# A separate buffer for the scaled activation, two roots moved, and feed-forward constants computed later: one post-norm transformer layer

## The reference

```python
x = layernorm(x + attention(x))     # 16 heads of 64, causal, softmax, W_out, b_out
x = layernorm(x + ffn(x))
def ffn(x):
    h = layernorm(x) * ln_gamma + ln_beta
    y = silu(h @ dequant(fc1_q, fc1_scales) + fc1_bias)     # 256 -> 1024
    return x + 0.5 * (y @ dequant(fc2_q, fc2_scales) + fc2_bias)     # 1024 -> 256
```

## Time and profile before

| | |
|---|---|
| median of 3 runs | 1814.26 us (1811.79 to 1815.73) |
| the profiled execution | 1813.47 us, of which the profile's span is 1811.4 us |
| PE busy | 1697.7 us (94%) |
| ACT busy | 1567.0 us (87%) |
| DVE busy | 1377.2 us (76%) |
| POOL busy | 1359.9 us (75%) |
| the chain that ended last | PE 66%; ACT 19%; POOL 5%; DVE 5%; issue 4% |
| attention | to about 1484 us |
| feed-forward | the rest, about 327 us |

### The profile page before, as it was taken

The page is one execution under the profiler, slowest core; times in us unless marked ns, Lnnn a source line. Parts: engine busy times, 40 slices in busy tenths (PEclk is TensorE's granted clock), DMA queues, the critical chain, the costliest instruction groups (busy, mean ns, idle before and its releaser), DMA issues.

```text
span 1811.4 us, 53985 instructions
## 1 busy us (share of the span) xinstructions
PE 1697.7 (94%) x21839; PEld 1153.9 (64%) x21839; DVE 1377.2 (76%) x3200; ACT 1567.0 (87%) x3244; POOL 1359.9 (75%) x833
## 2 busy tenths in 40 slices
PE   4799999999999999999999999989999989788886
PEld 2466666666666666666666666656666666565664
DVE  7979798978787879797989797979697825644443
ACT  3599999999999999999989999979999965657775
POOL 3498989898989898888889898979998971222222
PEclk9999999999999999999999999999999999999998
DMA  4013111111111112151212121201121511132200
GB/s 134 13 23 98 25 48 26 49 25 48 26 48 25 49 25 54 21 169 25 49 24 50 25 52 22 52 20 50 24 50 25 170 37 59 70 117 94 71 12 24
DMA packets 113207, 91.82 MB, mean 51 GB/s; under 512 B 73152, under 2 KB 100032, under 8 KB 111808
## 3 DMA queue, kind: packets, MB, share of 16 engines
q1 hardware_dynamic: 112960, 88.38, 18.0%
HBM read 33.82 MB, written 20.97 MB: 30 GB/s over the span
## 4 chain that ended last, share of the span: by engine, by line
PE 66%; ACT 19%; POOL 5%; DVE 5%; issue 4%; DMA 1%; SPq 0%; DVEq 0%; ACTq 0%
PE psum L1027 10%; PE psum L997 10%; PE psum L1031 10%; PE psum L968 7%; PE psum L1142 7%; PE psum L1055 5%; PE psum L1053 5%; PE psum L1057 5%; ACT p_parts L680 5%; ACT p_full L681 4%; PE psum L982 4%; POOL p_parts L576 4%; ACT kb L1229 2%; ACT p_full L1232 2%; PE psum L1033 1%
## 5 line engine op out<-in xcount | busy, mean ns | idle before, releaser
L576 POOL TENSOR_TENSOR p_parts<-p_full,p_parts 128x1024 f16<-128x1024 f32 (+1 forms) x640 | 1161.2, 1841 | 204.2 <-ACT p_full L681 202.3
L680 ACT ACTIVATE p_parts<-psum 128x512 f16<-128x512 f32 (+3 forms) x1280 | 727.3, 568 | 68.5 <-PE psum L1031 41.7
L681 ACT ACTIVATE p_full<-psum 128x512 f32<-128x512 f32 (+3 forms) x1280 | 734.9, 576 | 0.0
L747 DVE TENSOR_REDUCE row_max<-psum 128x1 f32<-128x512 f32 x768 | 484.6, 682 | 16.0 <-PE psum L997 12.9
L1053 PE MATMUL psum<-v,p_parts 128*128 128x65 f16 x4352 | 487.4, 193 | 7.6 <-POOL p_parts L576 4.7
L1055 PE MATMUL psum<-v,p_parts 128*128 128x64 f16 x4352 | 488.9, 194 | 0.0
L1057 PE MATMUL psum<-v,p_parts 128*128 128x65 f16 x4352 | 486.4, 193 | 0.0
L1053 PEld LDWEIGHTS psum<-v,p_parts 128*128 128x128 f16 x4352 | 406.7, 97 | 84.0 <-POOL p_parts L576 12.3
L1027 PE MATMUL psum<-qa,ka 128*128 128x512 f16 (+3 forms) x1280 | 445.3, 349 | 3.7 <-ACT p_full L681 3.4
L1055 PEld LDWEIGHTS psum<-v,p_parts 128*128 128x128 f16 x4352 | 402.8, 97 | 69.9 <-issue 0.6
L1031 PE MATMUL psum<-qb,kb 128*128 128x512 f16 (+3 forms) x1280 | 444.7, 348 | 2.3 <-DVE qb L760 2.2
(11 more groups left out here) (143 smaller groups left out, 2504.2 us busy)
## 6 DMA issues: line engine op xcount, KB each, us to landing
zT_dram<-z_T SPq DMA_DIRECT2D x16, 1024.0 KB, 4.5
qb<-qa SPq DMA_DIRECT2D x128, 64.0 KB, 2.0
ka<-ka SPq DMA_DIRECT2D x128, 64.0 KB, 1.9
shared_z<-zT_dram SPq DMA_DIRECT2D x4, 2048.0 KB, 8.4
x_hi<-zT_dram SPq DMA_DIRECT2D x4, 2048.0 KB, 8.8
shared_z<-xT_dram SPq DMA_DIRECT2D x8, 512.0 KB, 6.7
x_lo<-x_dram SPq DMA_DIRECT2D x8, 512.0 KB, 9.6
out_dram<-qa SPq DMA_DIRECT2D x8, 512.0 KB, 3.3
```

Of the source, the lines that this page charges most:

```text
L576: nc.gpsimd.tensor_tensor(p_lo[:, at % NP, cols], p_full[:, at % NP, cols], p_hi[:, at % NP, cols], ALU.subtract).then_inc(probs_split, 1)
L680: nc.scalar.activation(p_hi[:, at % NP, to], lane_bank(a)[:, P * f:QB], ACT.Exp, scale=1.0 / SCORE)
L681: nc.scalar.activation(p_full[:, at % NP, to], lane_bank(a)[:, P * f:QB], ACT.Exp, scale=1.0 / SCORE).then_inc(lane_read, 1)
L747: nc.vector.reduce_max(most, bank, AX.X).then_inc(ring_read, 1)
```

## The change

The full scaled copy of the activation gets a buffer of its own, `a_scaled`, in the area of the attention's low weight parts; GpSimd subtracts from it. The wait between the two copies (`a_high`) is gone. `fc1` waits for the silu that reads its PSUM bank and no longer for the copies. The roots of the last norms of blocks 0 and 6, which no output projection follows, stand behind f = 1 of the next block, and the silu preload behind them is gone; for blocks 1 to 5 and 7 root and preload stay (`projects(i)`, true for i = 1 to 5, is also the condition for the projection, which stays as it was). The constants' chain leaves `scales` and is computed by `constants()` on VectorE at the start of the feed-forward, ahead of `to_norms(0)`.

```diff
+        a_scaled = w_lo_all[:, 3 * D:3 * D + 2 * QB].rearrange("p (d t) -> p d t", d=2)
...
+        FIRST_PROJECTED = 1
...
                 if c0 == FFN_PEAK:
-                    w1_p, w2_p, gam_p, bet_p, b1_p = [powers[:, c0 + k:c0 + k + 1] for k in range(5)]
...
-                    step(nc.vector.tensor_scalar(bet_s[:, :], bet[:, :], h_scale[:, :], None, ALU.mult))
                     dve.sem_inc(scaled, 1)
                     dve.sem_inc(ring_read, 1)
                     return
...
+        def projects(i):
+            return FIRST_PROJECTED <= i < TOKB - 2
...
-                    nc.gpsimd.tensor_tensor(a_lo[:, f, :], a_full[:, f % 2, :], a_hi[:, f, :],
-                                            ALU.subtract).then_inc(a_split, 1)
+                    nc.gpsimd.tensor_tensor(a_lo[:, f, :], a_scaled[:, f % 2, :], a_hi[:, f, :], ALU.subtract).then_inc(a_split, 1)
...
-                pe.wait_ge(act_ready, i * FT + max(0, f - 1) + START)
+                pe.wait_ge(silu_done, i * FT + max(0, f - 1) + START)
...
-                if more == 2 and i:
+                if projects(i):
                     out_projection(i + 2)
...
-                    act.wait_ge(silu_done, at)
-                    nc.scalar.activation(a_hi[:, f, :], a_full[:, f % 2, :], ACT.Copy, scale=a_scale[:, :]).then_inc(a_high, 1)
-                    act.wait_ge(a_high, at)
-                    nc.scalar.activation(a_full[:, f % 2, :], a_full[:, f % 2, :], ACT.Copy,
-                                         scale=a_scale[:, :]).then_inc(act_ready, 1)
+                    act.wait_ge(silu_done, at + START)
+                    for dst in (a_hi[:, f, :], a_scaled[:, f % 2, :]):
+                        last = nc.scalar.activation(dst, a_full[:, f % 2, :], ACT.Copy, scale=a_scale[:, :])
+                    last.then_inc(act_ready, 1)
+                    if f == 1 and i and not projects(i - 1):
+                        root(3 * i + 1)
                     if more and f in ROOTS_AT:
                         root(3 * i + 2 + ROOTS_AT.index(f))
-                root(3 * i + 4 if more else 3 * i + 2)
-                if more:
+                if not more:
+                    root(3 * i + 2)
+                elif projects(i):
+                    root(3 * i + 4)
                     preload_silu(i + 1)
...
             def preload_silu(n):
-                act.wait_ge(preloaded, n + START)
+                act.wait_ge(preloaded, sum(projects(i) for i in range(n - 1)) + (n > 0) + START)
...
+            def constants():
+                step = Chain(ffn_consts, 0).done
...
+                step(nc.vector.tensor_scalar(bet_s[:, :], bet[:, :], h_scale[:, :], None, ALU.mult))
...
             dve.wait_ge(b2_halved, 1)
+            constants()
             to_norms(0, 0, 0)
```

More of the change, by code:

```diff
@@ L401, in program @@
         preloaded = sem("preloaded")
-        silu_done, a_high = sem("silu_done"), sem("a_high")
+        silu_done, ffn_consts = sem("silu_done"), sem("ffn_consts")
         stored = [sem("stored0"), sem("stored1")]
@@ L1214, in feed_forward_scalar @@
             act.sem_inc(act_ready, START)
+            act.sem_inc(silu_done, START)
             act.sem_inc(preloaded, START)
@@ L1283, in normalise @@
                 return last
+            def constants():
+                step = Chain(ffn_consts, 0).done
+                w1_p, w2_p, gam_p, bet_p, b1_p = [power[:, FFN_PEAK + k:FFN_PEAK + k + 1].bitcast(F32) for k in range(5)]
+                h_bits, a_bits = h_bound[:, 0:1].bitcast(I32), a_bound[:, 0:1].bitcast(I32)
+                step(nc.vector.tensor_scalar(h_bound[:, 1:2], bet_p, 2.0, None, ALU.mult))
+                step(nc.vector.scalar_tensor_tensor(out=h_bound[:, 0:1], in0=gam_p, scalar=32.0, in1=h_bound[:, 1:2],
+                                                    op0=ALU.mult, op1=ALU.add))
+                nc.vector.tensor_scalar(h_power[:, 0:1], h_bits, EXPONENT, None, ALU.bitwise_and)
+                step(nc.vector.tensor_scalar(h_power[:, 1:2], h_bits, EXPONENT, EXPONENT, ALU.bitwise_and, ALU.bitwise_xor))
+                h_p = h_power[:, 0:1].bitcast(F32)
+                nc.vector.tensor_scalar(h_scale[:, :], h_power[:, 1:2].bitcast(F32), 2.0 ** 12, None, ALU.mult)
+                nc.vector.tensor_scalar(u_inverse[:, :], w1_p, h_p, 2.0 ** -14, ALU.mult, ALU.mult)
+                step(nc.vector.tensor_scalar(a_bound[:, 1:2], b1_p, 2.0, None, ALU.mult))
+                step(nc.vector.scalar_tensor_tensor(out=a_bound[:, 0:1], in0=u_inverse[:, :], scalar=2.0 ** 24, in1=a_bound[:, 1:2],
+                                                    op0=ALU.mult, op1=ALU.add))
+                nc.vector.tensor_scalar(a_power[:, 0:1], a_bits, EXPONENT, None, ALU.bitwise_and)
+                step(nc.vector.tensor_scalar(a_power[:, 1:2], a_bits, EXPONENT, EXPONENT, ALU.bitwise_and, ALU.bitwise_xor))
+                nc.vector.tensor_scalar(a_scale[:, :], a_power[:, 1:2].bitcast(F32), 2.0 ** 12, None, ALU.mult)
+                nc.vector.tensor_scalar(o_inverse[:, :], w2_p, a_power[:, 0:1].bitcast(F32), 2.0 ** -15, ALU.mult, ALU.mult)
+                nc.vector.tensor_scalar(gam_s[:, :], gam[:, :], h_scale[:, :], None, ALU.mult)
+                step(nc.vector.tensor_scalar(bet_s[:, :], bet[:, :], h_scale[:, :], None, ALU.mult))
             NORMS, LAST = 9, 3
```

## The result

| | before | changed |
|---|---|---|
| median | 1814.17 us of 4 runs (1811.79 to 1815.73) | 1788.1 us of 4 runs (1781.76 to 1789.7) |
| ratio | | 0.9851, 95% interval 0.9823 to 0.9878 |
| profiled execution | 1813.47 us, span 1811.4 | 1786.58 us, span 1784.7 |

1785 was forecast, 1781 to 1794 as the range. The medians differ by 26.1 us, with an interval of 22 to 32, so they can't tell 26.1 from the forecast sum of 29.0; the traces can. Lines have moved: silu is line 1215, both copies are 1219 (the scaled one writes `w_lo`), GpSimd's subtraction is 1118, VectorE's low part of hT 1327, the root 1205, the copy of z 690, the first norm's line 1294 is 1306, and what was line 1327 is 1339.

What follows compares the result with a forecast made beforehand. ScalarE was taken to bound the feed-forward's groups, within a chain through GpSimd and TensorE. Gains of 12.1 + 4.0 + 5.2 + 7.7 = 29.0 us off 1813.47 gave 1784.5; with the median 0.8 higher, 1785, range 1781 to 1794.

Steps and rivals of the forecast that it cites:

- forecast sum of 29.0: Whole kernel: 12.1 + 4.0 + 5.2 + 7.7 = 29.0 us off the profiled execution's 1813.47.
- The pitch: Feed-forward groups: second copy 0.63 us behind the first instead of 0.75, saving 0.12 us a group, 0.96 a block.
- The order of GpSimd and VectorE: End of blocks 0 and 2 to 6: GpSimd's last subtraction starts first by 0.21 us, takes 1.15 us instead of 2.20.
- The cover for the waiting instruction: VectorE's line 1315 ends about 24.9 us; wanted at 25.0 in blocks 0 and 6, a projection later in others.
- The bank: First-layer work 1.4 us sooner on TensorE; hidden behind ScalarE in most groups, counting at the start of blocks 1 and 7.
- The deferred roots: Roots moved into blocks 1 and 7: 4.0 us gained in block 1 and 5.2 us in block 7.
- none over 1.5 but the first: Blocks 1 to 6: no TensorE idle time over 1.5 us apart from block 1's 2.4.
- Block 7's clock: Block 7: full clock supposed across an idle time of 2.4 us, giving 23.7 us instead of 28.86.
- so I take no fall: Block 7's new gap: clock stays full, as between 1768 and 1772, where TensorE was busy 1.90 of 4 us.
- the rival: Clock falls in block 7's new gap, costing up to 3 us: 1788, chance 0.11.
- another rival: GpSimd and VectorE do not change places: 7 x 1.05 = 7.4 us stay, 1792, chance 0.17.
- The constants: Attention unit 12: moving their chain gains 7.7 us, bounds 4.4 and 8.9; their new place costs nothing.

Runs made afterwards that it cites:

- the control with two waits: Changed kernel with the wait between the two copies put back for f = 0 and 1 alone; 1783.68 us, ratio 0.9846.
- the run with the bank undone: Changed kernel with the first layer waiting again for the copies of slice f - 2 instead of its silu; 1788.12 us, ratio 0.9854.
- changed kernel's second execution: Profiled execution from running the changed kernel again, unaltered; median 1784.92 us, ratio 0.9847 to the kernel before.

## Why the prediction was right

**The pitch.** Right, a little small: 0.14 us a group and not 0.12, with the wait between the copies worth the 0.12 (0.75 to 0.63) and the next silu 0.62 us behind the second copy instead of 0.63. From the first silu of a block to GpSimd's last subtraction it came to 1.13 us where 0.96 was forecast.

**The order of GpSimd and VectorE.** Right: forecast at a margin of 0.21 us, measured 0.24; 1.15 us and 1.99. This was the largest single uncertainty, and the control with two waits shows that the order, and not the pitch, was worth its 1.04 us. The cover for the waiting instruction held too, in blocks 0 and 6 narrowly: in block 0 it ended at 1536.56, and TensorE went on with block 1 at 1536.85 (0.29 us; 0.1 was forecast). In blocks 0 to 6 together 17.3 us against 16.1.

**The bank.** Half right. It does nothing in blocks 2 to 6, but the forecast had it count in blocks 1 and 7. That holds for the bank alone; in the changed kernel it is worth 1.4 us in block 7 and nothing in block 1, by the run with the bank undone.

**The deferred roots.** Block 1 from first matmul to last group: 28.1 forecast, 28.0 measured (1536.85 to 1564.84). Two loads and a root take 2.8 us here, without the 1.38 us of drain that the Trainium skill (ScalarE: Activation LUTs, What ACT_TABLE_LOAD costs) adds to each load; its 1.28 us for the load itself agrees. The largest waits of TensorE in blocks 1 to 6 are 2.19 us and, behind block 1's second root, 1.63, where the forecast found none over 1.5 but the first.

**Block 7's clock.** The step that failed is "so I take no fall". The reasoning went by a stretch with as much idle time in it that had kept its clock, from 1768 to 1772. That idle time was in two waits with work between them, 0.80 us and 1.73, the second running past the stretch's end:

```profile
1769.22 0.39 PE L1142 MATMUL psum<-w_raw_rest,p_full 128*128 128x256 f16 x2 [0.80 <-POOL p_parts L1132]
...
1772.44 0.39 PE L1142 MATMUL psum<-w_raw_rest,p_full 128*128 128x256 f16 x2 [1.73 <-POOL p_parts L1132]
```

The new gap is one wait of 2.19. In the profiled execution the clock fell behind it and the block took 25.6 us, not 23.7: 1.9 us, where the rival gave up to 3. The changed kernel's second execution took 23.9 with the same gap and no fall. It is a chance, then, but a high one: of the six profiled executions with a moved root behind f = 1 of block 7 (waits of 2.19 to 2.34 us), five show the fall. This rival should have had far more than its 0.11, and most of its price belonged in the sum. That the time came into the range all the same is owed to the range's width on that side, which had been drawn for another rival.

**The constants.** 7.7 forecast, 7.4 profiled, 7.6 by the median of the part alone. The forecast took the cost from TensorE's waits and the clock; that most of the chain's length was two tiny instructions held up by GpSimd (3.2 of 5.1 us) it did not see. The cost removed was itself partly chance: in the kernels with the buffer alone and the bank alone, unit 12 took 31.95 us and not 33.09, with its clock back sooner.

**What the forecast left out** is the clock fall at the attention's end, 2.4 us in the profiled execution. No run ties it to a part of the change, and the changed kernel's second execution went without it. It and block 7's 1.9 are 4.3 us lost, yet the sum is only 2.3 short of 29.0. On the other side stand 1.2 us more than forecast in blocks 0 to 6, mostly the pitch, and 1.3 us ahead of unit 12, where the two kernels are the same. That last part is luck. The constants and the rest of the attention took 0.5 back.

## What to carry to other kernels

When two engines share SBUF ports, look which one starts first and by how little: here 0.03 us the wrong way cost 1 us in each of seven blocks, and an edit worth 0.14 us a group turned it. A chain of tiny VectorE instructions is not free of this: one of them can wait out a whole GpSimd subtraction, as two did in unit 12. Work such an order out from how far each chain's start shifts, which can be done before anything is built. And when an instruction is moved out of the chain, look at what becomes part of the chain with it: table loads and transposes that ran beside a wait are free only there.

## What the runs showed of the hardware

The same idle time of TensorE brings a fall of its clock in one execution and not in another. Waits of up to 1.74 us in blocks 2 to 6 never brought one: the clock was 1.00 there in all 13 profiled executions. Those of 3.4 to 4.9 us at the start of blocks 1 and 7 brought one each time (eight of eight). In between, a wait of 2.19 to 2.34 us behind a moved root, it fell in ten of fifteen. Nor is the longest wait all that counts: at the attention's end it fell in five of the 13, with no single wait there over 1.1 us. The gap of block 7 brought it in the changed kernel's first profiled execution and not in its second, with the same instructions, waits and lengths on either side; block 1's gap of the same length did the opposite in the two (1.00 from 1537 to 1551 in the first; in the second 0.66 over the stretch here).

```profile
1544.00:1549.00 5.00, 5.00 (x23) 2.80 (x22) 4.42 (x13) 4.92 (x8) 2.71 (x2) 0.66 1.03 328
```

There it cost nothing, since ScalarE was the bound; in block 7 it cost 1.7 us (25.6 against 23.9), at the attention's end 2.4. The time ahead of the third copy of unit 12, through code that is the same in every kernel here, also differs by up to 5.3 us between the 13 executions (1188.07 to 1193.41); the clock in the first 100 us differs between them too. Together this is enough for the 8 us between the changed kernel's runs, though only two of those have a trace, 4.2 us apart. Blocks 2 to 5 repeat to 0.02 us, within an execution and between two of the same kernel. So a part worth two or three microseconds is better read from a stretch of the trace than from a median of four runs. What sets the chance was not tried.
